# First attention: the four maximum pieces of a head pair issued as two groups of two, with projection, turn and output transposes moved between the groups

## What is computed

```python
H, KV, DH = (16, 4, 64); G = H // KV
q = (x @ Wq).reshape(B, L, H, DH)
k = (x @ Wk).reshape(B, L, KV, DH)
v = (x @ Wv).reshape(B, L, KV, DH)
q = q * cos + _rotate_half(q) * sin
k = k * cos + _rotate_half(k) * sin
attn = softmax(einsum('bqkgd,bskd->bkgqs', q.reshape(B, L, KV, G, DH), k) * DH ** -0.5)
out = einsum('bkgqs,bskd->bqkgd', attn, v).reshape(B, L, H * DH) @ Wo
```

## Time and profile before

| what | value |
| --- | --- |
| time, median of 3 runs | 1281.28 us |
| lowest, highest | 1279.19, 1281.62 us |
| time of the profiled execution | 1279.61 us |
| its span, first to last instruction | 1277.8 us |
| busy share of the span: PE, DVE, POOL, ACT | 88%, 79%, 71%, 51% |
| mean granted TensorE clock | 0.953 |

### The profile page before, as it was taken

One profiled execution on the slowest core, in us unless ns is written; L12 is line 12 of the kernel. 1 busy time (PEld: TensorE's weight loads), 2 busy tenths in 40 slices (PEclk: granted clock), 3 DMA queues, 4 the chain that ended last, 5 costly groups with the idle time before them and its releaser, 6 DMA issues. The chain is left out here.

```text
span 1277.8 us, 30408 instructions
## 1 busy us (share of the span) xinstructions
PE 1119.9 (88%) x11049; PEld 708.2 (55%) x11049; DVE 1003.6 (79%) x1484; ACT 650.3 (51%) x1284; POOL 901.5 (71%) x744
## 2 busy tenths in 40 slices
PE   3689999989999998999999999766887989897975
PEld 2245565555565564565564565454544666665854
DVE  4588968967977976877877879746858999998884
ACT  2245545634545544645645645425765655554442
POOL 3388878867879877869878969612437797877721
PEclk9699999999999998999999999977987999999998
DMA  5212212112112112112111211110000000000000
GB/s 150 50 39 52 48 30 52 46 34 52 39 27 64 39 27 51 42 39 51 40 39 43 47 39 37 38 30 0 1 2 0 1 1 1 1 9 10 9 17 25
DMA packets 48726, 42.21 MB, mean 33 GB/s; under 512 B 7973, under 2 KB 46904, under 8 KB 48568
## 3 DMA queue, kind: packets, MB, share of 16 engines
q1 hardware_dynamic: 48136, 39.35, 12.8%
q10 hardware_dynamic: 432, 0.79, 0.2%
HBM read 6.42 MB, written 2.10 MB: 7 GB/s over the span
## 5 line engine op out<-in xcount | busy, mean ns | idle before, releaser
L505 ACT ACTIVATE a_probs<-a_ps_s 128x512 f32<-128x512 f32 x512 | 303.9, 597 | 325.9 <-PE a_ps_s L417 321.4
L736 POOL TENSOR_TENSOR a_p_lo<-a_probs 128x512 f16<-128x512 f32 x384 | 420.1, 1116 | 32.8 <-ACT a_probs L505 29.6
L664 DVE TENSOR_REDUCE a_nmx<-a_ps_m 128x2 f32<-128x1024 f32 x256 | 311.1, 1216 | 32.7 <-PE a_ps_m L400 31.8
L433 PE MATMUL a_ps_o<-a_v_hi,a_probs 128*128 128x65 f16 x2048 | 243.7, 196 | 16.1 <-DVE a_p_lo L671 8.4
L434 PE MATMUL a_ps_o<-a_v_lo,a_probs 128*128 128x64 f16 x2048 | 241.0, 194 | 0.0
L435 PE MATMUL a_ps_o<-a_v_hi,a_p_lo 128*128 128x65 f16 x2048 | 240.7, 195 | 0.0
L433 PEld LDWEIGHTS a_ps_o<-a_v_hi,a_probs 128*128 128x128 bf16 x2048 | 189.9, 99 | 88.1 <-issue 58.7
L415 PE MATMUL a_ps_s<-a_qq,a_kk 128*128 128x512 f16 x512 | 197.3, 385 | 9.3 <-issue 6.3
L434 PEld LDWEIGHTS a_ps_o<-a_v_lo,a_probs 128*128 128x128 bf16 x2048 | 191.6, 99 | 25.0 <-issue 1.3
L417 PE MATMUL a_ps_s<-a_qq,a_k_l 65*128 65x512 f16 x512 | 198.0, 387 | 0.0
L435 PEld LDWEIGHTS a_ps_o<-a_v_hi,a_p_lo 128*128 128x128 f16 x2048 | 191.2, 98 | 0.0
(11 more groups left out here) (238 smaller groups left out, 2130.8 us busy)
## 6 DMA issues: line engine op xcount, KB each, us to landing
a_qq<-a_rhi SPq DMA_DIRECT2D x128, 128.0 KB, 2.4
a_qq<-a_rlo SPq DMA_DIRECT2D x128, 64.0 KB, 2.0
a_kk<-a_rhi SPq DMA_DIRECT2D x64, 64.0 KB, 2.0
a_k_l<-a_rlo SPq DMA_DIRECT2D x32, 64.0 KB, 2.0
out_x<-x_sb SPq DMA_DIRECT2D x8, 256.0 KB, 2.3
a_qq<-a_nmT SPq DMA_DIRECT2D x64, 2.0 KB
a_probs<-in_wq ACTq DMA_DIRECT2D x1, 512.0 KB, 5.0
a_wo<-in_wo SPq DMA_DIRECT2D x1, 512.0 KB, 11.9
```

Source lines behind the costliest of these rows:

```text
L433: nc.tensor.matmul(out, hi, v_hi[:, b % 2, kt, g, 0:65], start=(kt == 0), stop=False)
L505: nc.scalar.activation(probs[:, p % 2, kt, h, :], ps_s[:, i % 2, :], ACT.Exp, scale=DH0 ** -0.5).then_inc(exp_done, 1)
L664: nc.vector.tensor_reduce(nmx[:, p % 2, i:2 * QT:QT], ps_m[:, n % 2, :, :], axis=X, op=ALU.max, negate=True).then_inc(free[n % 2], 1)
L736: nc.gpsimd.tensor_tensor(p_lo[:, p % 2, kt, h, :], pr, pr.bitcast(BF16)[:, 1:2 * L:2], ALU.subtract).then_inc(lo_pool, 1)
```

## The change

The one list for all engines is replaced by tables of places in ticks, 32 to a step, one table for each engine; an engine's items are sorted by tick, and at one tick by the order of `KINDS`. No instruction is added or taken away. The tables put B0 and B1 at one tick and B2 and B3 at one tick. For a step s in which nothing of a batch element falls, the items come out in this order (the number after the sign is the pair, counted from s; items in which an engine has nothing to do are left out):

The diff, with the removed list and the long row of weight rounding items cut, and one of the five alike calls of `run` kept beside the first:

```diff
--- before.py
+++ after.py
@@ -44,95 +44,69 @@
 LOOP_FROM, PERIOD, ROUNDS = 3, 16, 3
 
 
-def pipeline():
...
-        steps[s] = [it for sl in slots for it in sl]
+PAIR_AT = {
+    "PE": {"C": (0, 4, 8, 12, 16, 20, 24, 28), "B": (-64, -64, -48, -48), "A": (-88,), "M": (-24,), "O": (88,), "D": (24, 28, 32, 36, 40, 44, 48, 52)},
+    "ACT": {"C": (0, 4, 8, 12, 16, 20, 24, 28), "RH": (-80,), "MX": (-28,), "M": (-24,), "O": (88,)},
+    "DVE": {"A": (-88,), "B": (-64, -64, -48, -48), "L": (4, 8, 12, 16, 20, 24, 28, 32), "D": (24, 28, 32, 36, 40, 44, 48, 52)},
+    "POOL": {"RS": (-84,), "RL": (-76,), "L": (4, 8, 12, 16, 20, 24, 28, 32)},
+    "SP": {"RL": (-76,), "M": (-24,)},
+}
+SEQ_AT = {
+    "PE": {"HT": (-176,), "K": (-152, -140), "V": (-108,), "W": (320,)},
+    "ACT": {"HT": (-176,), "KH": (-140, -132), "V": (-108,)},
+    "DVE": {"LN": (-204, -200, -196), "K": (-152, -140), "V": (-108,), "W": (320,)},
+    "POOL": {"LN": (-204, -200, -196), "HL": (-172,), "KS": (-144, -136), "KL": (-136, -132), "W": (320,)},
+    "SP": {"KL": (-136, -132)},
+}
+ONCE_AT = {
+    "PE": ((-4, ("G",)), (2108, ("FT", 0)), (2140, ("FT", 1))),
+    "ACT": ((-4, ("G",)), (2108, ("FT", 0)), (2140, ("FT", 1))),
+    "DVE": ((-176, ("WS",)), (1992, ("FQ", 0, 0)), (1996, ("FQ", 0, 1)), (2000, ("FQ", 0, 2)), (2004, ("FQ", 0,
...
+            ("FQ", 1, 7)), (2100, ("FQ", 1, 8)), (2104, ("FQ", 1, 9))),
+    "POOL": (),
+    "SP": ((1980, ("FL",)),),
+}
+KINDS = ("C", "W", "B", "A", "RS", "RH", "RL", "MX", "M", "O", "D", "L", "LN", "HT", "HL", "K", "KS", "KH", "KL", "V")
+
+
+def first_order(engine):
+
+    items = []
+
+    def put(tick, it):
+        items.append((tick, len(items), it))
+
+    for kind in KINDS:
+        for i, at in enumerate(PAIR_AT[engine].get(kind, ())):
+            for p in range(B * PAIRS):
+                put(32 * p + at, (kind, p) + ({"C": (i,), "B": (i,), "L": (i,), "D": divmod(i, QT)}.get(kind, ())))
+        for i, at in enumerate(SEQ_AT[engine].get(kind, ())):
+            for b in range(B):
+                put(256 * b + at, (kind, b) + ((i,) if kind in ("LN", "K", "KS", "KH", "KL") else ()))
+    for tick, it in ONCE_AT[engine]:
+        put(tick, it)
+    steps = {s: [] for s in range(FIRST, LAST + 1)}
+    for tick, _, it in sorted(items, key=lambda x: x[:2]):
+        steps[tick // 32].append(it)
     return steps
 
 
 def layer0_attention(nc, x_sb, modT, mod_f, gate_bc, ident, ffn_w, dram):
-    steps = pipeline()
+    order = {e: first_order(e) for e in ("PE", "ACT", "DVE", "POOL", "SP")}
 
     job, rope = {}, {}
     for s in range(FIRST, LAST + 1):
-        for it in steps[s]:
+        for it in order["PE"][s]:
             if it[0] in ("A", "K", "B", "M", "O", "V", "HT", "W", "G", "FT"):
                 job[it] = len(job)
-            if it[0] in ("RS", "KS"):
+            if it[0] in ("A", "K"):
                 rope[it[1:]] = len(rope)
     ropes_in_order = list(rope)
-    JOBS16 = job[("O", LOOP_FROM - 2 + PERIOD)] - job[("O", LOOP_FROM - 2)]
-    ROPE16 = rope[(LOOP_FROM + 3 + PERIOD,)] - rope[(LOOP_FROM + 3,)]
+    JOBS16 = job[("O", 1 + PERIOD)] - job[("O", 1)]
+    ROPE16 = rope[(6 + PERIOD,)] - rope[(6,)]
     assert JOBS16 % 2 == 0 and ROPE16 % 2 == 0
 
     with ExitStack() as ex:
@@ -271,7 +245,8 @@
             def seq_index(self, b):
                 return b if self.i is None else self.i * 2 + b
 
-        def run(eng, item):
+        def run(eng, name, item):
+            steps = order[name]
             for s in range(FIRST, LOOP_FROM):
                 for it in steps[s]:
                     item(Turn(eng, None), it)
@@ -341,7 +316,7 @@
                             sp.dma_start(f_w[f][0:96, (3 * a + 2) * D:(3 * a + 3) * D],
                                          name[256:INNER, :]).then_inc(ld_f, 16)
                         sp.dma_start(f_w[f][:, 6 * D:FW], names[2]).then_inc(ld_f, 16)
-            run(sp, item)
+            run(sp, "SP", item)
 
         @block.tensor
         def _(pe):
...
@@ -739,7 +714,7 @@
-            run(pool, item)
+            run(pool, "POOL", item)
```

More of the change, by code:

```diff
@@ L465, in item @@
                     last.then_inc(full[n % 2], 1)
-            run(pe, item)
+            run(pe, "PE", item)
         @block.scalar
@@ L533, in item @@
                                          ps_m[:, n % 2, :, 0:INNER], ACT.Copy).then_inc(free[n % 2], 1)
-            run(act, item)
+            run(act, "ACT", item)
         @block.vector
@@ L692, in item @@
                     quantize(*it[1:])
-            run(dve, item)
+            run(dve, "DVE", item)
         @block.gpsimd
```

## The result

| | before | after |
| --- | --- | --- |
| median of 4 runs each | 1280.78 us | 1264.58 us |
| lowest, highest | 1279.19, 1281.62 | 1259.41, 1266.76 |
| profiled execution, and its span | 1279.61, 1277.8 | 1259.41, 1257.6 |
| mean granted TensorE clock | 0.953 | 0.955 |

The ratio is 0.9869, with a 95% interval of 0.9837 to 0.9901: faster by 16.2 us. Run again beside other kernels on another occasion, the same kernel gave 1265.48 (1262.70 to 1270.02, six runs), ratio 0.9884 (0.9862 to 0.9905).

A forecast was written before the change was run, and what follows sets the result against it. A plain step of 10.13 us was taken as bound by a ring of PE and DVE, neither alone. 37 steps at 0.54 save 20.0: 1281.28 - 20.0 = 1261.3, with 0.7 given back 1262; range 1256 to 1276.

The forecast's parts named there:

- The load in a group is hidden: On PE the second B's weight load hides, so it costs 0.22: 0.19 saved in a group, 0.38 a step.
- Rival (a): The second B's load in a group is not hidden: step 9.79, saving 12.6 us, time 1269; chance 0.22.
- The ring opened: Plain step: B3 no longer waits for B2's reduction on DVE but for M's copy on ACT; 0.16 goes.
- Rival (c): Slower through POOL: turn 1.0 us later, L3 late by 1.2 holds D00, time 1287; chance 0.10.
- The plain step: PE's step without W, keys or V falls from 10.13 to 9.59 us, 0.54 saved in each of 37.
- O's edge: O behind B2's reduction on DVE, the tightest edge with nothing to spare: 0.02 a step, 0.7 us given back.
- DVE's need of 9.2 a step: DVE's own work in a plain step, about 9.2 us, fits into 9.59 with 0.4 to spare.
- W's step: Step with W and HT: B1 loses 0.76, HT comes 0.3 later, 0.38 back; ends 0.25 late, 19.45 us.
- The keys' step: Step with key projections: K0 waits 1.06 for A's turn, K1 0.87 for B2; 14.1 instead of 13.32 us.
- V's step: Step with V: POOL's queue ends no later, so 1.0 of lateness is absorbed; 11.9 instead of 12.90 us.
- The sum: 37 plain steps at 0.54 save 20.0 us; W, keys and V steps together count 0; 0.7 given back, 1262.
- Fill and end of the attention stay as they are: The attention's start and end, and everything behind it, unchanged, since no instruction there changes.

The follow-up runs named there:

- e9: Changed kernel with the second group undone, B2 and B3 apart, B0 and B1 still together: 1281.65 us, plain step 9.89.
- Experiments 1 and 3: 1: groups without the moves of A, M, O, 1363.44 us; 3: changed kernel with M, A or O moved back, 1328.57, 1278.18, 1298.37, or second group split, 1281.65.
- Experiment 4: Changed kernel with SP alone edited, the twelve key transfers issued behind the next maxima's transfer instead of ahead: 1258.62 us, ratio 0.9848.
- experiment 5: Changed kernel with W issued behind the first group and C1 on PE, and at the same tick on DVE and POOL: 1307.44 us, ratio 1.0226.

## Why the prediction was right, and where its steps failed

The forecast was 1262, the median is 1264.58, 2.6 above it. That the profiled execution, forecast at 1259.6, took 1259.41 is luck: 3.5 us of its gain lie behind the attention, where nothing was changed. By its own steps:

- **The load in a group is hidden: right.** B1 to D02 and B0 together take 0.54, so the second B costs 0.22. Rival (a) had 0.32. e9 shows the size from the other side, 0.19 for one group. TensorE's weight loads show the hiding itself, to be read against the earlier trace rows: of the 40 loads of B now only every second pair lies bare, and the idle time ahead of them is 4.3 us instead of 9.4.

```profile
L375 PEld LDWEIGHTS a_ps_m<-a_kk,a_rhi 64*128 64x128 f16 x40 | 1.1, 94 | 4.3 <-issue 2.1 <-DVE a_arena L624 2.1
```

  The rule of the Trainium skill that was weighed in the prediction (TensorE: Matmul & The Clock Gate, "Part 3: Packing small matmuls") would have meant rival (a), 1269; these rows disagree with it as it is worded, for 64-row loads as well as for 128-row ones.
- **The ring opened: right.** No wait in the plain step; DVE idle 0.38 ahead of the turn (0.4 forecast), D00 waits for nobody. Experiments 1 and 3 show that it's the moves that open it, and what each is worth. Rival (c) didn't come: POOL still idles 0.7 a step ahead of RS (3.5 us in the five).
- **The plain step: 9.59 forecast, 9.65 measured.** O's edge, priced at 0.02, was no edge. A has M behind it instead of a D, and M has another shape: A takes 1.38 instead of 1.30. 0.48 is saved in a step, not 0.54.
- **DVE's need of 9.2 a step: too high, and harmless.** Its busy time fell from 46.85 to 40.75. Of the 6.1, some 5 are the low parts (ten at 0.53 less each), the rest pieces of other steps. The last section shows why they got shorter, which the text hadn't foreseen. The tightest edge thus had more to spare than the laying out gave it.
- **W's step: 19.45 forecast, 19.33 measured,** away from the loop's turns. B1 starts 0.97 after B0 (about 1 forecast). The 0.25 is near by luck in part: the terms named for it, 0.76 and 0.3 less 0.38, make 0.68. HT's wait didn't grow by 0.3; it is 0.72 where it was 0.78.
- **The keys' step: 14.1 forecast, 14.34 measured,** with K0 waiting 0.87 and K1 0.86 (1.06 and 0.87 forecast), K0 from 0.13 behind the turn's end (0.06 forecast).
- **V's step: the step that failed.** The text had "the 1.0 of lateness is absorbed there, and the step comes out at 11.9", and of transfers only that "SP's order is the same". It measured 12.40 in the mean, 12.99 at most. The order on SP is the same, but its timing isn't: keys that come later hold the maxima's transfer until 406.62, and the next C waits 1.13. Experiment 4 takes that away and finds 11.70 everywhere. So the lateness is absorbed within the step, as said, and comes back through SP, a queue that the text had passed over at no cost. Of the -7.0 forecast for these steps, 3.7 are missing.
- **The sum.** Of 19.8 forecast (20.0 with the special steps rounded to nothing), 2.0 are missing in the plain steps, 1.4 with the keys and 3.7 with V; 1.7 too much was put down for W, and 3.1 came at both ends, that weren't looked at. That is 17.5, from the first C0 to the last.
- **"Fill and end of the attention stay as they are": wrong, as is W's sum as a mere 7 x 0.25.** The first step of W's kind, in the fill (a norm and HT, no W), takes 18.38 instead of 15.25. There A waits for B0's reduction, which stands on DVE behind the norm's last part, as W does in experiment 5; before, the same norm held PE for 2.43 only, ahead of B1:

```profile
83.56 0.61 PE L353 MATMUL a_ps_m<-a_hT_hi,a_arena 128*128 128x512 f16 x1 [5.26 <-DVE a_nmx L639]
```

  The two in which the loop turns over take 0.8 and 1.0 less, the one in which it ends 1.6 less. These cancel by chance. Of the 4.2 at both ends, 2.6 lie in the very last step, where PE waited for a low part on DVE before and doesn't after:

```profile
813.65 0.19 PE L433 MATMUL a_ps_o<-a_v_hi,a_probs 128*128 128x65 f16 x1 [2.88 <-DVE a_p_lo L671]
```

  The steps in which the loop turns over aren't steady: in the rerun the keys' steps at the loop's two turns take 17.11 and 16.56 from C0 to C0, against 15.75 and 15.90. Why these turns vary between executions wasn't tried and stays open.

So the mechanism and the size of the plain step stand; V's step gave half of what was hoped from it, and the two ends, not forecast, gave most of that back. That the sum came out within 3 us owes this much to luck.

## What to carry to other kernels

Two products in a group save the cost of the change of shape once. But where results go to two places in turn, a group fills both, and the jobs behind it wait for the slower engine that reads them out. Here grouping paid only when the items behind each group were chosen so that those reductions had ended before they came (1.063 of the time without the moves, 0.987 with them). When a step gets shorter, look at each in-order queue for an item that is small and urgent and stands behind many that aren't; a transfer queue counts as one, here mostly at 0.5 to 0.7 us for each transfer. After the plain step is settled, the steps that come once in a while are worth the same care: here the last 17.7 us came from them, by moving twelve numbers in a table.

## What the runs showed of the hardware

**A low part on DVE waits for the instruction that POOL has under way, and the other way round.** L646 (L671 before) is the same instruction everywhere, with two operands in SBUF. The timeline of VectorE and GpSimd after, in a plain step:

```profile
433.28 0.68 DVE L646 TENSOR_TENSOR a_p_lo<-a_probs 128x512 f16<-128x512 f32 x1
```

```profile
433.44 1.65 POOL L694 TENSOR_TENSOR a_rot<-a_arena 128x512 f32<-128x512 f32 x1 [0.43 <-DVE a_arena L624]
```

And before, where POOL is at work first:

```profile
437.91 1.04 POOL L736 TENSOR_TENSOR a_p_lo<-a_probs 128x512 f16<-128x512 f32 x1
438.13 1.37 DVE L671 TENSOR_TENSOR a_p_lo<-a_probs 128x512 f16<-128x512 f32 x1
```

In the first pair POOL is idle as DVE begins, and DVE takes 0.68; POOL's RS, which begins inside it, takes 1.65, where it had a mean of 1.27 before. In the second, POOL still has 0.82 to go when DVE begins, and DVE takes 1.37, that is 0.82 + 0.55. This holds throughout: of the 71 low parts after that begin with more than 0.15 left of one of POOL's, every one takes what is left plus 0.55, within 0.01, and of 112 such before, 105; the other seven meet POOL's small reciprocal root (L713) and take about 0.68. RS takes what is left of DVE's plus 1.13 (0.52 in the row above). The Trainium skill, SBUF — State Buffer, section "Who interferes with whom", says that a DVE instruction with two SBUF inputs contends with a GpSimd instruction that reads SBUF, and that the order of issue decides which of them blocks; the runs agree. So the price isn't fixed: it is what the other still has to do. In the plain steps after, one low part begins while POOL waits for the turn and the other as POOL's RL ends: that made them 0.5 us shorter, and RS 0.4 longer.

**A change of shape costs PE about 0.1 each way,** and M's eight columns count as one: A took 1.38 ahead of M and 1.30 ahead of a D. **The granted clock fell to 0.50** behind a wait of 4.37 us for which PE did nothing, in experiment 5, and cost W 3 us more.
